# Eigenvectors of a normalised Laplacian inside a two-layer graph network: one twisted factorisation instead of two, three refinements instead of two, a shorter last QR sweep

## Chip, cores and metric

The kernel runs on 1 core of a Trainium2 chip. The metric is the device time of an execution in microseconds (us); lower is better.

## The reference, cut to what matters

Input are x (128 batches of 128 nodes by 128 features, f32) and one 128x128 adjacency matrix. The first layer needs the eigenvectors of its normalised Laplacian, with the signs that the library's routine gives them, the second is a graph convolution followed by LSTM cells over windows of 1 to 4 nodes:

```python
deg = jnp.sum(A, axis=0) + jnp.sum(A, axis=1) - jnp.diagonal(A)
d_inv_sqrt = jnp.where(deg > 0, jax.lax.rsqrt(deg), 0.0)
L_norm = d_inv_sqrt[:, None] * (jnp.diag(deg) - A) * d_inv_sqrt[None, :]
_, U = jnp.linalg.eigh(L_norm)
out = relu(jnp.einsum('mn,bnd->bmd', U.T, relu(layernorm(x))) @ W1 + b1) @ W2 + b2
x = x + jnp.einsum('nm,bmd->bnd', U, out)
# then layer norm, two mixing layers with adj, LSTM cells for p = 1..4, and a second residual sum
```

## The kernel before, in words

The program for each engine is written out by hand with semaphores; no planner sets the order. It has two halves. The second half, the batch part, runs over 128 batches in 8 rounds of 4 streams of 4 batches; its first matmul is L735, which waits for `eig_done`, and the diff does not touch it. The first half computes the eigenvectors U (and UT) for all batches at once:

- **Tridiagonal form.** 127 Householder steps (`householder(k, before)` on DVE, lines 910 to 972). A step is a chain over three engines: DVE makes the new row x (L963), PE spreads it over the partitions (L618, L620), ACT takes the square root of the sum of squares (L442) and half the absolute pivot (L443), DVE forms u (L926), PE multiplies it with A (L623, L625), and DVE computes the next row and updates A (L952 to L972). L930 copies the sum of squares, plus a tiny number, out of PSUM; `prepare_sign` (L979, L980) and `prepare_row` (L986) prepare the next step's sign vector. L986 stands behind the last update of A, L972. ACT fills its spare time with the layer norm's statistics.
- **The leaf's sign.** After 16 steps DVE hands the leading 16x16 block to POOL (`leaf_ready`). POOL runs 16 sweeps of a QR iteration on it, in a loop of 88 instructions (lines 335 to 416); each sweep looks for the active block (L347 to L364), computes a shift (L365 to L375), forms the pivots d - shift (L377), and multiplies the parity `PAR` by the sign of the first (L379, L383). A recurrence of 15 pairs L386, L388 follows, then products over 16 elements (L390 to L415), with one long `pow` at L403. At each turn the loop clears its semaphore. Only `PAR` is used afterwards: L417 passes it to DVE with `leaf_sign`.
- **Eigenvalues and vectors.** DVE, beside POOL, runs two Sturm counts (L1120 to L1151) and then `twisted` twice: a factorisation from both ends for 4 levels of splitting at once, 127 steps of small instructions (L1203, L1209), and then wide instructions over 4 levels of 128 elements (L1212 to L1255). The first call corrects the eigenvalues by a Rayleigh quotient (L1245, L1259 to L1262), the second gives the vectors V4.
- **Refinement.** The vectors are turned back by PE (L608 to L709) and refined twice against the Laplacian (L1291 to L1340), PE and DVE in turn. The signs follow from V4 and from POOL's parity: in the last refinement DVE waits for `leaf_sign` before L1360, forms the row of signs in M[9] (L1363), applies the last step (L1366) and the signs (L1369 to L1385). L1382 and L1385 release the batch part.
- **PE and ACT in between** build the product of reflectors, turn the LSTM weights, and normalise and multiply x by W1 in place; they end before DVE's vectors. ACT's L517 waits for DVE's L1266.

Semaphore waits of one engine are in order: what stands behind a waiting instruction waits with it.

Of the kernel before, what the change touches and what calls it, by code (L numbers as in the profile page):

```python
# [19 lines left out]
TINY = 1e-30  # L20
QR_PER = 88
RAYLEIGH_CLIP = 4e-5
REGULAR = 1e-12
REFINES = 2

# [34 lines left out]
def build(nc, t_in, out):  # L60
    with ExitStack() as ctx:
# [117 lines left out]
        rs_out = sem("rs_out")  # L179
        st1, st2, tw1, tw2 = sem("st1"), sem("st2"), sem("tw1"), sem("tw2")  # L180
        pool_s = sem("pool_s")
# [19 lines left out]
        def half_x(k):  # L201
            return sc[:, 28 + k % 2:29 + k % 2]
# [98 lines left out]
        def _(pool):  # L301
# [33 lines left out]
            TS = nc.gpsimd.tensor_scalar  # L335
            with nc.gpsimd.Fori(0, QR_SWEEPS) as k:
                pool.sem_clear(pool_q)
                q = Tally(pool_q)

                def op(ins):  # L340
                    q.did(ins)
                    q.last(pool)

                def go(ins):
                    return q.did(ins)

                go(TT(y16[:, 0:15], d16[:, 0:15], d16[:, 1:16], ALU.mult))  # L347
# [27 lines left out]
                op(TT(SIG, SIG, S(OG), ALU.subtract))  # L375

                op(TS(am, d16, SIG, 1e-15, ALU.subtract, ALU.add))  # L377

                go(TS(T0, am[:, 0:1], 0.0, -2.0, ALU.is_ge, ALU.mult))  # L379
                n_par = q.n  # L380
                n_rho = go(TT(rho[:, 0:1], am[:, 0:1], neg16[:, 0:1], ALU.pow))
# [33 lines left out]
                op(TT(d16[:, LEAF - 1:LEAF], SIG, gam[:, LEAF - 1:LEAF], ALU.add))  # L415
                assert q.n == QR_PER, q.n
            nc.gpsimd.tensor_copy(S(PAR), S(PAR)).then_inc(leaf_sign, 1)  # L417
            pool.wait_ge(ln_var, 3)
# [4 lines left out]
        def _(act):  # L423
# [15 lines left out]
            for k in range(STEPS):  # L439
                t = k + 1  # L440
                act.wait_ge(s_ready, k + 1)
                nc.scalar.activation(two_sigma(k), banks[7][:, 1:2], ACT.Sqrt, scale=4.0).then_inc(sigma_ready, 1)  # L442
                nc.scalar.activation(half_x(k), banks[7][:, 0:1], ACT.Abs, scale=0.5).then_inc(sigma_ready, 1)  # L443
                act.wait_ge(a_ready, k + 1)
                nc.scalar.activation(S_(ACOL), A[:, t:t + 1], ACT.Copy, scale=below[:, t:t + 1]).then_inc(acol_ready, 1)
                if t + 1 < N:
                    act.wait_ge(xb_ready, k + 1)
                    nc.scalar.activation(uB[:, k % 2, t + 1:N], banks[0][:, t + 1:N], ACT.Copy).then_inc(row_ready, 1)
                act.wait_ge(sg_ready, k + 1)
                act.wait_ge(sigma_ready, 2 * k + 1)  # L450
# [149 lines left out]
        def _(pe):  # L600
# [116 lines left out]
            for r in range(REFINES):  # L717
                mms((B[3], Lap[:], U[:]))
                also((B[5], U[:], U[:]))
                mms((B[6], ones[:], V4[:, 1, :]))  # L720
                mms((B[4], U[:], M[0]))
                mms((B[1], ones[:], M[2]))
                if r == REFINES - 1:
                    mms((banks[0][:, 0:2 * N], ones[:], diag2))
                mms((B[3], UT[:], M[5]))
                also((B[2], M[5], UT[:]))
# [118 lines left out]
        def _(dve):  # L845
# [66 lines left out]
            def householder(k, before):  # L912
# [8 lines left out]
                sigma2, sg = two_sigma(k), sign(k)  # L921
                x_t, s = banks[7][:, 0:1], banks[7][:, 1:2]

                dve.wait_ge(sigma_ready, 2 * k + 1)
                dve.wait_ge(hv, before)
                V.scalar_tensor_tensor(out=u_c, in0=S(SGE), scalar=sigma2, in1=x_c,  # L926
                                       op0=ALU.mult, op1=ALU.add).then_inc(u_ready, 1)

                dve.wait_ge(sigma_ready, 2 * k + 2)
                n_st = step(V.tensor_scalar(S(ST), s, TINY, None, ALU.add))  # L930
                V.tensor_scalar(sg, x_t, 0.0, 0.5, ALU.is_ge, ALU.subtract).then_inc(sg_ready, 1)
                dve.wait_ge(hv, n_st)
                n_den = step(V.scalar_tensor_tensor(out=S(DEN), in0=half_x(k), scalar=sigma2, in1=S(ST),
# [12 lines left out]
                if t + 1 < N:  # L946
# [22 lines left out]
                                                   in1=banks[1][:, live(k)], op0=ALU.mult, op1=ALU.subtract))  # L969
                n_sge1 = prepare_sign(k + 1) if k + 1 < STEPS else None  # L970
                dve.wait_ge(hv, max(n_a, n_wb))
                V.scalar_tensor_tensor(out=A[:, live(k)], in0=wB[:, live(k)], scalar=S(HU), in1=A[:, live(k)],  # L972
                                       op0=ALU.mult, op1=ALU.add).then_inc(a_ready, 1)
                return prepare_row(k + 1, n_sge1) if k + 1 < STEPS else None

            def prepare_sign(k):

                dve.wait_ge(x_ready, k + 1)
                n_sge1 = step(V.tensor_scalar(S(SGE1), ident[:, N:N + 1], 0.0, 0.5, ALU.is_ge, ALU.subtract))  # L979
                step(V.tensor_tensor(UC[:, k, 1:2], ident[:, N:N + 1], below[:, k + 1:k + 2], ALU.mult))  # L980
                return n_sge1

            def prepare_row(k, n_sge1):
# [4 lines left out]
            before = prepare_row(0, prepare_sign(0))  # L988
            for k in range(LEAF):
# [195 lines left out]
            TWO = [slice(0, 2), slice(2, 4)]  # L1185
            LEAST, GSUM, NORM, INV, RQ = 56, 60, 20, 24, 36


            def twisted(sem, vectors):
                for l in range(LEVELS):  # L1190
# [47 lines left out]
                for l in range(LEVELS):  # L1238
# [3 lines left out]
                                                      ALU.mult, ALU.add))  # L1242
                for l in range(LEVELS):
                    if not vectors:
                        go(V.tensor_tensor_reduce(out=GAM[:, l, :], in0=GAM[:, l, :], in1=ONE[:, l, :], scale=1.0,  # L1245
                                                  scalar=0.0, op0=ALU.mult, op1=ALU.add, accum_out=S(GSUM + l)))
                for h in TWO:
# [9 lines left out]
                t.last(dve)  # L1257
                if not vectors:
                    op(V.reciprocal(S(RQ, LEVELS), S(NORM, LEVELS)))  # L1259
                    op(V.tensor_tensor(S(RQ, LEVELS), S(RQ, LEVELS), S(GSUM, LEVELS), ALU.mult))  # L1260
                    op(V.tensor_scalar(S(RQ, LEVELS), S(RQ, LEVELS), RAYLEIGH_CLIP, -RAYLEIGH_CLIP, ALU.min, ALU.max))
                    op(V.tensor_tensor(lam4[:], lam4[:], S(RQ, LEVELS), ALU.add))  # L1262

            twisted(tw1, False)
            twisted(tw2, True)
            V.tensor_copy(S(41), S(NORM)).then_inc(rs_in, 1)  # L1266
            n_31 = go(V.scalar_tensor_tensor(out=S(31), in0=ident[:, 64:65], scalar=wrow[:, 0, 64:65], in1=ident[:, 63:64],
                                             op0=ALU.mult, op1=ALU.add))
            largest = tell(V.tensor_tensor(S(30), lam4[:, 0:1], ident[:, N - 1:N], ALU.mult))  # L1269
            CC, ZZ, LF, SIGN, LFA, LFB = 44, 47, 50, 54, 55, 40  # L1270
            for l in range(LEVELS - 1):
# [19 lines left out]
            for r in range(REFINES):  # L1291
# [50 lines left out]
                if r == 0:  # L1342

                    op(V.tensor_tensor(S(ZZ, 3), S(ZZ, 3), S(INV + 1, 3), ALU.mult))
                    go(V.tensor_scalar(S(ZZ, 3), S(ZZ, 3), S(43), None, ALU.is_le))
                    go(V.tensor_scalar(S(CC, 3), S(CC, 3), 0.0, None, ALU.is_lt))
                    go(V.tensor_scalar(S(LF), V4[:, 0, 0:1], 0.0, None, ALU.is_gt))
                    op(V.tensor_scalar(S(LF + 1), V4[:, 0, 0:1], 0.0, None, ALU.is_lt))
                    for l in (2, 1, 0):
# [176 lines left out]
```

## Time and profile before

| | before |
|---|---|
| median of 3 runs | 1515.49 us (1513.96 to 1518.14) |
| the profiled execution | 1516.81 us, span 1515.1 us |
| busy share PE / DVE / ACT / POOL | 79% / 73% / 62% / 34% |
| granted TensorE clock, mean | 0.939 |
| span until the batch part's first matmul | 660.71 us |

The span runs from the first to the last instruction; the execution's own time includes what lies around it. Shares are averages over two halves that are bound by different engines: in the first PE is seldom busy, in the second almost always. An instruction's row gives its start, its duration and, in brackets, how long its engine had been idle and who released it.

### The profile page before, as it was taken

The page shows a single profiled execution, that of the slowest core. Times are in us where ns is not written, and L with a number is a line of the kernel's source. Part 1 is how long each engine was busy: PE and PEld are TensorE (multiplying, and loading weights), DVE is VectorE, ACT ScalarE, POOL GpSimd, SP SyncE. Part 2 cuts the span into 40 slices and gives each one's busy share as a digit, 9 for nine tenths or more (in the row PEclk, how much of TensorE's full clock was granted, in tenths as well). Part 3 has the DMA queues.
Part 4 walks back from the last instruction along what each step waited for, and adds up shares of the span by engine and source line. Part 5 has one row for each costly group of instructions (what it writes and reads, how often), then busy time and mean ns, then how long its engine had stood idle before and what let it go on. Part 6 is the DMA issues. An engine that isn't in the chain of part 4 may idle for free.

```text
span 1515.1 us, 26850 instructions
## 1 busy us (share of the span) xinstructions
PE 1196.2 (79%) x7121; PEld 1069.9 (71%) x7121; DVE 1107.1 (73%) x5944; ACT 943.2 (62%) x3339; POOL 508.6 (34%) x1426
## 2 busy tenths in 40 slices
PE   5777777777536400179999999999999999999998
PEld 4566666666435300168789899898998989989897
DVE  8999999999999999958747656455564554645545
ACT  4666666666349600012478687786877868778676
POOL 0288888888888888830000200000000000000000
PEclk9999999999869855579999999999999999999999
DMA  9300000000000000003100000000000000000001
GB/s 269 79 1 1 1 1 1 1 1 1 1 1 1 1 0 0 1 28 105 36 1 2 28 0 28 0 0 28 0 28 0 0 28 0 26 2 0 28 1 29
DMA packets 43630, 28.80 MB, mean 19 GB/s; under 512 B 1520, under 2 KB 39440, under 8 KB 43536
## 3 DMA queue, kind: packets, MB, share of 16 engines
q1 hardware_dynamic: 43536, 27.81, 6.7%
q14 instruction: 67, 0.55, 0.1%
q8 instruction: 27, 0.44, 0.1%
HBM read 19.42 MB, written 8.39 MB: 18 GB/s over the span
## 4 chain that ended last, share of the span: by engine, by line
PE 52%; POOL 33%; issue 7%; DVE 6%; ACT 2%; POOLq 0%; ACTq 0%; DVEq 0%
PE bank L815 13%; PE bank L805 10%; POOL leaf L388 9%; PE bank L810 8%; PE bank L818 7%; POOL leaf L386 6%; POOL leaf L403 3%; PE bank L735 2%; PE bank L787 2%; PE bank L779 2%; PE bank L743 2%; PE bank L773 2%; PE bank L750 2%; PE bank L758 2%; ACT BIG L552 1%
## 5 line engine op out<-in xcount | busy, mean ns | idle before, releaser
L815 PE MATMUL bank<-spare,wT 128*128 128x256 f32 (+2 forms) x1408 | 311.3, 321 | 0.0
L552 ACT ACTIVATE PV<-bank,bias 128x256 f32<-128x256 f32 (+2 forms) x704 | 304.0, 435 | 0.0
L552 ACT ACTIVATE BIG<-bank,bias 128x128 f32<-128x128 f32 (+2 forms) x544 | 227.6, 418 | 121.0 <-PE bank L818 101.9
L815 PEld LDWEIGHTS bank<-spare,wT 128*128 128x128 f32 x1408 | 234.8, 191 | 13.2
L805 PE MATMUL bank<-spare,wT 128*128 128x128 f32 (+2 forms) x1088 | 228.1, 320 | 4.1 <-DVE spare L1446 2.7
L1432 DVE TENSOR_TENSOR BIG<-BIG,PV 128x128 f32<-128x128 f32 (+2 forms) x192 | 63.0, 328 | 205.9 <-ACT BIG L552 205.9
L805 PEld LDWEIGHTS bank<-spare,wT 128*128 128x128 f32 x1088 | 168.7, 190 | 22.5 <-DVE spare L1446 9.1
L818 PE MATMUL bank<-spare,wT 128*128 128x128 f32 (+2 forms) x768 | 169.7, 303 | 0.0
L810 PE MATMUL bank<-spare,wT 128*128 128x128 f32 (+2 forms) x768 | 141.6, 307 | 3.8 <-DVE spare L1444 1.4
L618 PE MATMUL bank<-ident 128*128 128x2 f32 x254 | 74.3, 362 | 88.6 <-DVE ident L963 87.5
L388 POOL TENSOR_TENSOR leaf<-leaf 128x1 f32<-128x1 f32 x240 | 136.7, 570 | 20.0
L560 ACT ACTIVATE spare<-spare 128x256 f32<-128x256 f32 (+2 forms) x352 | 134.4, 382 | 6.9 <-DVE spare L1435 6.9
L618 PEld LDWEIGHTS bank<-ident 128*128 128x128 f32 x254 | 63.6, 311 | 99.6 <-DVE ident L963 98.2
L1429 DVE TENSOR_TENSOR spare<-BIG,PV 128x256 f32<-128x256 f32 (+2 forms) x160 | 60.8, 380 | 95.7 <-ACT PV L552 95.6
L818 PEld LDWEIGHTS bank<-spare,wT 128*128 128x128 f32 x768 | 125.2, 191 | 3.3
L810 PEld LDWEIGHTS bank<-spare,wT 128*128 128x128 f32 x768 | 113.8, 191 | 14.2 <-DVE spare L1444 10.9
L386 POOL TENSOR_SCALAR leaf<-leaf 128x1 f32<-128x1 f32 x240 | 93.3, 389 | 23.4
L610 PE MATMUL bank<-ones,sc 128*128 128x1 f32 x2 | 0.6, 348 | 120.5 <-DVE sc L1269 120.5
L442 ACT ACTIVATE sc<-bank 128x1 f32<-128x1 f32 x127 | 21.7, 171 | 116.1 <-PE bank L618 116.0
L623 PE MATMUL bank<-A,UC 128*128 128x127 f32 (+63 forms) x254 | 87.5, 442 | 7.3 <-DVE UC L926 0.8
L1209 DVE SCALAR_TENSOR_TENSOR PV<-RC,m,PV 128x4 f32<-128x4 f32 x508 | 90.6, 220 | 0.0
L610 PEld LDWEIGHTS bank<-ones,sc 128*128 128x128 f32 x2 | 0.5, 313 | 120.6 <-issue 120.6
(405 smaller groups left out, 3000.8 us busy)
## 6 DMA issues: line engine op xcount, KB each, us to landing
spare<-in_x SPq DMA_DIRECT2D x32, 256.0 KB, 3.8
out<-X SPq DMA_DIRECT2D x32, 256.0 KB, 2.4
spare<-in_L_gnn_Wih SPq DMA_DIRECT2D x4, 256.0 KB, 5.2
spare<-in_L_gnn_Whh SPq DMA_DIRECT2D x4, 256.0 KB, 4.6
W<-in_L_gnn_W SPq DMA_DIRECT2D x2, 64.0 KB, 2.7
Wg<-in_L_gnn_Wg SPq DMA_DIRECT2D x2, 64.0 KB, 2.4
adj<-in_adj SPq DMA_DIRECT2D x1, 64.0 KB, 2.0
X<-in_x SPq DMA_DIRECT2D x4, 0.5 KB, 17.0
```

Of the source, the lines that this page charges most:

```text
L386: op(TS(am[:, i + 1:i + 2], rho[:, i:i + 1], ne16[:, i:i + 1], am[:, i + 1:i + 2], ALU.mult, ALU.add))
L388: op(TT(rho[:, i + 1:i + 2], am[:, i + 1:i + 2], neg16[:, 0:1], ALU.pow))
L552: last = nc.scalar.activation(gate_out[q][i][:, 0:T], gate(i, q, T), ACT.Tanh if q == GATE_G else ACT.Sigmoid, bias=bias[:, at:at + 1])
L560: nc.scalar.activation(tS[i][:, 0:T], cS[i][:, 0:T], ACT.Tanh).then_inc(tanh_ready[i], 1)
L618: nc.tensor.matmul(banks[7][:, 0:2], x_wide, ident[:, t:N + 1:N - t], start=True, stop=True).then_inc(s_ready, 1)
L623: nc.tensor.matmul(banks[1][:, live(k)], u_c.to_broadcast([N, N]), A[:, live(k)], start=True, stop=True).then_inc(pb_ready, 1)
L805: last = nc.tensor.matmul(gate(i, q, T), wT[:, 0, p - 1, q * D:(q + 1) * D], xt, start=True, stop=(j == 0))
L810: last = nc.tensor.matmul(gate(i, q, T), wT[:, 1, p - 1, q * D:(q + 1) * D], hS[i][:, 0:T], start=False, stop=True)
L815: last = nc.tensor.matmul(gate(i, q, T), wT[:, 0, p - 1, q * D:(q + 1) * D], xt, start=True, stop=(j == 0))
L818: last = nc.tensor.matmul(gate(i, q, T), wT[:, 1, p - 1, q * D:(q + 1) * D], hS[i][:, 0:T], start=False, stop=True)
L1209: s.did(V.scalar_tensor_tensor(out=nx, in0=RC[:, last + lane:last + lane + live], scalar=M[2][:, row:row + 1], in1=nx, op0=ALU.mult, op1=A ...
L1432: V.tensor_tensor(gI[i][:, 0:T], gI[i][:, 0:T], gG[i][:, 0:T], ALU.mult).then_inc(cell_part[i], 1)
```

## The change

- POOL's 16 sweeps are written out instead of looped, and the last ends after its shift: it computes the first pivot alone and its sign, and the final product of `PAR` signals `leaf_sign`.
- In a Householder step ACT makes the copy of the sum of squares (`S(ST)`) as its third instruction, L930 on DVE goes, and DVE waits for all three ACT results before L931. The sign vector for the next step (L986) is formed before the last update of A, not behind it.
- `twisted` runs once, without the Rayleigh correction, and there are three refinements. A new scalar `LINKED` (whether the first split is coupled) masks the last test of the signs, through a third block in the diagonal matrix that PE spreads, and the test's threshold is 0 instead of 1e-4.

```diff
-REFINES = 2
+REFINES = 3
...
-            with nc.gpsimd.Fori(0, QR_SWEEPS) as k:
-                pool.sem_clear(pool_q)
-                q = Tally(pool_q)
...
+            for k in range(QR_SWEEPS):
                 go(TT(y16[:, 0:15], d16[:, 0:15], d16[:, 1:16], ALU.mult))
...
+                if k == QR_SWEEPS - 1:
+                    op(TS(am[:, 0:1], d16[:, 0:1], SIG, 1e-15, ALU.subtract, ALU.add))
+                    op(TS(T0, am[:, 0:1], 0.0, -2.0, ALU.is_ge, ALU.mult))
+                    break
                 op(TS(am, d16, SIG, 1e-15, ALU.subtract, ALU.add))
...
-            nc.gpsimd.tensor_copy(S(PAR), S(PAR)).then_inc(leaf_sign, 1)
+            TS(S(PAR), T0, 1.0, S(PAR), ALU.add, ALU.mult).then_inc(leaf_sign, 1)
...
                 nc.scalar.activation(half_x(k), banks[7][:, 0:1], ACT.Abs, scale=0.5).then_inc(sigma_ready, 1)
+                nc.scalar.activation(S_(ST), banks[7][:, 1:2], ACT.Copy, bias=TINY).then_inc(sigma_ready, 1)
...
-                act.wait_ge(sigma_ready, 2 * k + 1)
+                act.wait_ge(sigma_ready, 3 * k + 1)
...
                 if r == REFINES - 1:
-                    mms((banks[0][:, 0:2 * N], ones[:], diag2))
+                    mms((banks[0][:, 0:3 * N], ones[:], diag3))
...
-                dve.wait_ge(sigma_ready, 2 * k + 2)
-                n_st = step(V.tensor_scalar(S(ST), s, TINY, None, ALU.add))
+                dve.wait_ge(sigma_ready, 3 * k + 3)
                 V.tensor_scalar(sg, x_t, 0.0, 0.5, ALU.is_ge, ALU.subtract).then_inc(sg_ready, 1)
-                dve.wait_ge(hv, n_st)
...
-                n_sge1 = prepare_sign(k + 1) if k + 1 < STEPS else None
+                following = prepare(k + 1) if k + 1 < STEPS else None
                 dve.wait_ge(hv, max(n_a, n_wb))
                 V.scalar_tensor_tensor(out=A[:, live(k)], in0=wB[:, live(k)], scalar=S(HU), in1=A[:, live(k)],
                                        op0=ALU.mult, op1=ALU.add).then_inc(a_ready, 1)
-                return prepare_row(k + 1, n_sge1) if k + 1 < STEPS else None
-
-            def prepare_sign(k):
+                return following
+
+            def prepare(k):
...
-            twisted(tw1, False)
-            twisted(tw2, True)
+
+            twisted(tw)
...
                 if final:
-                    go(V.tensor_scalar(diag2[:, 0:N], I, S(LFA), None, ALU.mult))
-                    signs = tell(V.tensor_scalar(diag2[:, N:2 * N], I, S(LFB), None, ALU.mult))
+                    go(V.tensor_scalar(diag3[:, 2 * N:3 * N], I, S(LINKED), None, ALU.mult))
+                    go(V.tensor_scalar(diag3[:, 0:N], I, S(LFA), None, ALU.mult))
+                    signs = tell(V.tensor_scalar(diag3[:, N:2 * N], I, S(LFB), None, ALU.mult))
...
                     op(V.tensor_tensor(S(ZZ, 3), S(ZZ, 3), S(INV + 1, 3), ALU.mult))
+                    op(V.tensor_scalar(S(LINKED), S(ZZ), S(43), None, ALU.is_gt))
...
-                else:
+                elif final:
                     hear(signs)
...
+                    go(V.tensor_tensor(S(TEST), S(SIGN), S(LINKED), ALU.mult))
+                    op(V.tensor_tensor(M[8], banks[0][:, 2 * N:3 * N], M[9], ALU.mult))
...
-            n_r = go(V.tensor_tensor(M[2], B[6], M[9], ALU.mult))
+            n_r = go(V.tensor_tensor(M[2], B[6], M[8], ALU.mult))
...
-            n_c = go(V.tensor_tensor(S(53), banks[5][:, 0:1], S(SIGN), ALU.mult))
+            n_c = go(V.tensor_tensor(S(53), banks[5][:, 0:1], S(TEST), ALU.mult))
```

## Rows read from the trace of the kernel before

**Rows 1.** The page, part 4: the chain that ended last, shares of the span by engine.
```profile
PE 52%; POOL 33%; issue 7%; DVE 6%; ACT 2%; POOLq 0%; ACTq 0%; DVEq 0%
```

**Rows 2.** List of waits to 661 us: engine, line, waited for: total, times, longest.
```profile
ACT sc L517 <- DVE sc L1266: 119.5, 1, 119.5
DVE sc L1360 <- POOL leaf L417: 3.4, 1, 3.4
```

**Rows 3.** Timeline, POOL: start us, us, engine, line, operation, xcount [idle before].
```profile
64.31 0.21 POOL L347 TENSOR_TENSOR leaf<-leaf 128x15 f32<-128x15 f32 x1 [0.25 <-POOL leaf L333]
...
580.02 0.21 POOL L347 TENSOR_TENSOR leaf<-leaf 128x15 f32<-128x15 f32 x1 [0.46 <-POOL leaf L415]
...
625.22 1.31 POOL L377 TENSOR_SCALAR leaf<-leaf 128x16 f32<-128x16 f32 x1
...
657.87 0.18 POOL L417 COPY leaf<-leaf 128x1 f32<-128x1 f32 x1 [0.23 <-POOL leaf L415]
```

**Rows 4.** The chain in order of time: start us, us, what; POOL's L403, one a sweep.
```profile
95.58 2.78 POOL leaf L403
...
575.30 2.79 POOL leaf L403
610.98 2.79 POOL leaf L403
...
653.37 2.79 POOL leaf L403
```

**Rows 5.** Groups of POOL: count, busy us, mean ns of one, idle us before.
```profile
L379 POOL TENSOR_SCALAR leaf<-leaf 128x1 f32<-128x1 f32 x16 | 4.3, 270 | 1.4
```

**Rows 6.** Timeline of one early Householder step, DVE and, last, PE.
```profile
18.35 0.34 DVE L972 SCALAR_TENSOR_TENSOR A<-wB,sc,A 128x126 f32<-128x126 f32 x1
18.61 0.15 DVE L986 TENSOR_TENSOR sc<-sc,ident 128x1 f32<-128x1 f32 x1
18.87 0.22 DVE L926 SCALAR_TENSOR_TENSOR UC<-sc,ident 128x1 f32<-128x1 f32 x1
19.00 0.15 DVE L930 TENSOR_SCALAR sc<-bank 128x1 f32<-128x1 f32 x1
19.19 0.22 DVE L933 SCALAR_TENSOR_TENSOR sc<-sc 128x1 f32<-128x1 f32 x1
19.97 0.22 DVE L952 SCALAR_TENSOR_TENSOR sc<-bank,sc 128x1 f32<-128x1 f32 x1
...
19.14 0.79 PE L623 MATMUL bank<-A,UC 128*128 128x125 f32 x2
```

**Rows 7.** Timeline, DVE: second factorisation's first, L1266 after its last, last refinement's first and last.
```profile
560.28 0.34 DVE L1191 TENSOR_SCALAR PV<-D,lam 128x128 f32<-128x128 f32 x1
...
635.70 0.15 DVE L1266 COPY sc<-sc 128x1 f32<-128x1 f32 x1
...
648.13 0.29 DVE L1297 TENSOR_TENSOR U<-U,bank 128x128 f32<-128x128 f32 x1
...
654.44 0.28 DVE L1358 COPY m<-bank 128x128 f32<-128x128 f32 x1
```

**Rows 8.** Timeline, POOL: L386 beside factorisation's start, in the quiet stage, beside refinements.
```profile
560.58 1.46 POOL L386 TENSOR_SCALAR leaf<-leaf 128x1 f32<-128x1 f32 x1
...
590.76 0.33 POOL L386 TENSOR_SCALAR leaf<-leaf 128x1 f32<-128x1 f32 x1
...
596.27 0.34 POOL L386 TENSOR_SCALAR leaf<-leaf 128x1 f32<-128x1 f32 x1
...
636.24 0.56 POOL L386 TENSOR_SCALAR leaf<-leaf 128x1 f32<-128x1 f32 x1
...
648.28 0.34 POOL L386 TENSOR_SCALAR leaf<-leaf 128x1 f32<-128x1 f32 x1
```

**Rows 9.** Timeline, DVE: the first instruction behind L1363.
```profile
658.60 0.29 DVE L1366 TENSOR_TENSOR U<-U,bank 128x128 f32<-128x128 f32 x1
```

**Rows 10.** Windows, 660 to 665 us: busy of each engine, PEclk, DMA share, GB/s.
```profile
660.00:665.00 5.00, 4.29 (x20) 4.29 (x21) 1.01 (x7) 1.16 (x2) 0.00 (x0) 0.50 0.00 0
```

More of the change, by code:

```diff
@@ L20 @@
 TINY = 1e-30
-QR_PER = 88
-RAYLEIGH_CLIP = 4e-5
 REGULAR = 1e-12
-REFINES = 2
+REFINES = 3
 BATCH, D = 128, 128
@@ L179, in build @@
         rs_out = sem("rs_out")
-        st1, st2, tw1, tw2 = sem("st1"), sem("st2"), sem("tw1"), sem("tw2")
+        st1, st2, tw = sem("st1"), sem("st2"), sem("tw")
         pool_s = sem("pool_s")
@@ L237, in build @@
         DOUBLINGS = 6
-        diag2 = BIG[:, 5 * GW:5 * GW + 2 * N]
+        diag3 = BIG[:, 5 * GW:5 * GW + 3 * N]
         def squares_done(e):
@@ L335, in _, with go @@
             TS = nc.gpsimd.tensor_scalar
-            with nc.gpsimd.Fori(0, QR_SWEEPS) as k:
-                pool.sem_clear(pool_q)
-                q = Tally(pool_q)
[L340 to L345, printed above, removed]
+            def go(ins):
+                return q.did(ins)
+            for k in range(QR_SWEEPS):
                 go(TT(y16[:, 0:15], d16[:, 0:15], d16[:, 1:16], ALU.mult))
@@ L375, in _ @@
                 op(TT(SIG, SIG, S(OG), ALU.subtract))
+                if k == QR_SWEEPS - 1:
+                    op(TS(am[:, 0:1], d16[:, 0:1], SIG, 1e-15, ALU.subtract, ALU.add))
+                    op(TS(T0, am[:, 0:1], 0.0, -2.0, ALU.is_ge, ALU.mult))
+                    break
                 op(TS(am, d16, SIG, 1e-15, ALU.subtract, ALU.add))
-                go(TS(T0, am[:, 0:1], 0.0, -2.0, ALU.is_ge, ALU.mult))
-                n_par = q.n
+                n_par = go(TS(T0, am[:, 0:1], 0.0, -2.0, ALU.is_ge, ALU.mult))
                 n_rho = go(TT(rho[:, 0:1], am[:, 0:1], neg16[:, 0:1], ALU.pow))
@@ L415, in _ @@
                 op(TT(d16[:, LEAF - 1:LEAF], SIG, gam[:, LEAF - 1:LEAF], ALU.add))
-                assert q.n == QR_PER, q.n
-            nc.gpsimd.tensor_copy(S(PAR), S(PAR)).then_inc(leaf_sign, 1)
+            TS(S(PAR), T0, 1.0, S(PAR), ALU.add, ALU.mult).then_inc(leaf_sign, 1)
             pool.wait_ge(ln_var, 3)
@@ L921, in householder @@
                 sigma2, sg = two_sigma(k), sign(k)
-                x_t, s = banks[7][:, 0:1], banks[7][:, 1:2]
-                dve.wait_ge(sigma_ready, 2 * k + 1)
+                x_t = banks[7][:, 0:1]
+                dve.wait_ge(sigma_ready, 3 * k + 1)
                 dve.wait_ge(hv, before)
@@ L980, in prepare_sign @@
                 step(V.tensor_tensor(UC[:, k, 1:2], ident[:, N:N + 1], below[:, k + 1:k + 2], ALU.mult))
-                return n_sge1
-            def prepare_row(k, n_sge1):
                 dve.wait_ge(hv, n_sge1)
                 return step(V.tensor_tensor(S(SGE), S(SGE1), ident[:, k + 1:k + 2], ALU.mult))
-            before = prepare_row(0, prepare_sign(0))
+            before = prepare(0)
             for k in range(LEAF):
@@ L1185, in _, with twisted @@
             TWO = [slice(0, 2), slice(2, 4)]
-            LEAST, GSUM, NORM, INV, RQ = 56, 60, 20, 24, 36
-            def twisted(sem, vectors):
+            LEAST, NORM, INV = 56, 20, 24
+            def twisted(sem):
                 for l in range(LEVELS):
@@ L1242, in twisted @@
                                                       ALU.mult, ALU.add))
[L1243 to L1246, printed above, removed]
                 for h in TWO:
@@ L1257, in twisted @@
                 t.last(dve)
[L1258 to L1262, printed above, removed]
-            twisted(tw1, False)
-            twisted(tw2, True)
+            twisted(tw)
             V.tensor_copy(S(41), S(NORM)).then_inc(rs_in, 1)
@@ L1269, in _ @@
             largest = tell(V.tensor_tensor(S(30), lam4[:, 0:1], ident[:, N - 1:N], ALU.mult))
-            CC, ZZ, LF, SIGN, LFA, LFB = 44, 47, 50, 54, 55, 40
+            CC, ZZ, LINKED, LF, SIGN, LFA, LFB, TEST = 44, 47, 37, 50, 54, 55, 40, 38
             for l in range(LEVELS - 1):
@@ L1373, in _ @@
             hear(by_row)
-            n_r = go(V.tensor_tensor(M[2], B[6], M[9], ALU.mult))
+            n_r = go(V.tensor_tensor(M[2], B[6], M[8], ALU.mult))
             hear(by_col)
-            n_c = go(V.tensor_tensor(S(53), banks[5][:, 0:1], S(SIGN), ALU.mult))
+            n_c = go(V.tensor_tensor(S(53), banks[5][:, 0:1], S(TEST), ALU.mult))
             dve.wait_ge(v_, n_r)
-            n_r = go(V.tensor_scalar(M[2], M[2], 1e-4, -2.0, ALU.is_gt, ALU.mult))
+            n_r = go(V.tensor_scalar(M[2], M[2], 0.0, -2.0, ALU.is_gt, ALU.mult))
             dve.wait_ge(v_, n_c)
-            n_c = go(V.tensor_scalar(S(53), S(53), 1e-4, -2.0, ALU.is_gt, ALU.mult))
+            n_c = go(V.tensor_scalar(S(53), S(53), 0.0, -2.0, ALU.is_gt, ALU.mult))
             dve.wait_ge(v_, n_r)
```

## The prediction, made before the changed kernel was run

> **What bounds the kernel now.** I read the chain of waits first: PE holds 52% of it and POOL 33% [rows 1]. In the part before 661 us (the eigenvectors) the reader is to see that POOL, not DVE, is last. DVE is busy almost without a break there, but the list of waits shows that it stood 3.4 us before L1360 until POOL's L417 gave it the leaf's sign [rows 2]. So the two engines run side by side and POOL ends 3.4 us later: taking work from DVE alone gains nothing. ACT waited 119.5 us for DVE's L1266, so it has slack. After L1382 everything is the batch part, bound by PE; the diff does not touch it, so it moves as one block with the moment at which U is ready.
>
> POOL's timeline gives its chain: it starts with DVE's leaf values, the first sweep's L347 is at 64.31, the last sweep passes L377 at 625.22, and L417 ends at 658.05 (657.87 + 0.18) [rows 3]. That is one serial chain of 16 sweeps.
>
> **The change, part by part.**
>
> 1. **Last sweep only to its pivot.** What ran from L377's start to L417's end, 658.05 - 625.22 = 32.8 us, goes [rows 3]. In its place come three instructions on one element, each waiting for the one before: 3 x 270 ns, the mean of L379, plus two gaps of 0.09 us (1.4 us of idle time over 16) [rows 5], 1.0 us. **-31.8 us**, all on the path.
>
> 2. **Sweeps written out.** At each turn of the loop POOL stands 0.46 us before L347 [rows 3], where a dependent instruction stands 0.09 [rows 5]. 15 x 0.37 = **-5.6 us**. Ends: 0, if the 0.46 is not the branch and the semaphore clear; +4.6 if fresh code costs something. For the latter the trace has one hint: the loop's first pass, whose code has never run, took 31.27 us from L347 to L403 (64.31 to 95.58), a later quiet one 30.96 (580.02 to 610.98) [rows 3, 4]; 0.31 x 15 = 4.6. I take the full gain, since the first pass also ran beside Householder steps. The Trainium skill (Runtime: NRT & Kernel Launch, Instruction fetch mechanics) says that instructions stream in blocks of 16 KiB whose crossing is mostly hidden, and that a taken branch is what disturbs this; by it the full gain stands too, and its "mostly" is what the slow rival below would need.
>
> 3. **Householder steps.** POOL starts after 16 of them; the other 111 run on DVE beside POOL and are worth nothing at the end. In an early step [rows 6] L986 starts 0.26 after L972 and L926 0.26 after that. With L986 put ahead of L972, it costs its short issue slot (some 0.1) and L926 follows L972 at 0.26: about 0.14 earlier. With L930 on ACT, DVE's L933 no longer waits for it: it can start 0.07 behind L931 rather than 0.19 behind L930, 0.12 sooner. But PE's L623 ends at 19.93 and L952 starts at 19.97: PE moves with L926 only, so 0.14 is kept. ACT's new copy issues behind L442 and L443 and ends about when L931 could start. I take 0.13 a step, 16 x 0.13 = **-2.1 us**. Ends: -4.2 (0.26 a step, both gains), and +1.0 if DVE now waits 0.06 a step for ACT's third result.
>
> 4. **One twisted factorisation less, one refinement more.** On DVE the removed one is 635.70 - 560.28 = 75.4 us, about as the second; a refinement is 654.44 - 648.13 = 6.3 us and 0.9 for PE's product [rows 7], which the next one has nothing to cover with. DVE would then be ready for the sign at 654.7 - 75.4 + 7.2 = 586, and at some 570 with all 127 steps shorter. POOL's new end is 620, so DVE now waits 35 to 50 us at L1360: this part is worth **0 by itself**, hidden by POOL. ACT's work before L517 keeps at least 119.5 - 75.4 - 16 = 28 us of slack.
>
> 5. **What DVE's wide instructions do to POOL.** In a quiet stage (DVE on 4-element instructions) a pair L386, L388 takes (596.27 - 590.76) / 5 = 1.10 us; beside the refinement (648.28 - 636.24) / 10 = 1.20 [rows 8]. The sweep that met the second factorisation's wide end and the refinements took 653.37 - 610.98 = 42.4 us against 35.7 before it [rows 4]: 6.7 lost, 1.0 of it beside refinements, so 5.7 to the factorisation's end. In the sum so far, all that was lost after 625 went with term 1. Now the surviving sweeps meet the one factorisation end as before, not the second one's set-up (L386 took 1.46 instead of 0.34 at 560.58, -1.1 [rows 8]), and all of the preparation and three refinements, 27 us x 0.09 = +2.4. **+1.3 us.** Ends: -1, and +11 (27 us at the end-stage's rate, 5.7 in 12). I take the rate of the refinement itself, since it is the same work. The Trainium skill (SBUF — State Buffer, Who interferes with whom) has a rule against this change: a DVE instruction with two SBUF inputs and a GpSimd instruction that reads SBUF exclude each other for a whole instruction. By that rule alone the added refinement would cost POOL up to several us; the rows above show 1.2 us lost for 12 us of refining.
>
> 6. **Tail after the sign.** L1363 is followed by a product with the new PSUM columns (0.29, as L1366 [rows 9], with a gap and the TEST product in front), all on the path: **+0.4 us**. LINKED and the third diagonal lie in DVE's slack.
>
> 7. **PE's clock.** From 660 to 665 the granted clock was 0.50 with PE busy 4.3 of 5 us [rows 10], that is 1.2 GHz at the start of the batch part. PE will now have stood longer before it, but it is already at the low level: 0. Ends: -1 and +2, by when the clock rises.
>
> Sum: -31.8 - 5.6 - 2.1 + 1.3 + 0.4 = **-37.8 us**. The profiled execution took 1516.81 us for a span of 1515.1; it gives 1479.0. The median of the runs, 1515.49, is 1.3 lower: **1477.7 us**.
>
> **Rivals.**
> - *Denser DVE work stalls POOL*: the sweeps beside the refinements lose at the rate of the factorisation's end, +9.7 over term 5: 1487. For: single POOL instructions reach 1.46 [rows 8]; against: the 1.20 a pair.
> - *The change does less than it says*: turn gap and Householder order give nothing: -31.8 + 1.3 + 0.4 = -30.1: 1485. For: the 0.46 is only attributed to the turn, and PE, ACT and DVE are nearly tied in a step [rows 6].
> - *DVE becomes last*: it would need 35 us more on DVE, and the floor of its own path is 658.1 - 586 = 72 us below today's: 1443. Only if POOL's written-out sweeps were much quicker.
> - *Slower than before, by POOL's written-out code*: POOL is the bound, and a sweep has 74 waits, 15 x 74 + 25 = 1135 in all. If fresh code stretched each gap of 0.09 by half, that is +51 us: 1529. It decides from 38 / 1135 = 0.033 us a wait. For: POOL has never run written-out code of this length here. Against: the loop's first pass, 0.31 us slower for 74 waits, and DVE's own written-out stream.
>
> **How the numbers follow.** A measurement of this kernel can tell about 0.3%, 4.5 us. The forecast case (POOL's chain, terms near those taken, 1472 to 1483) gets 0.69; denser stalls 0.13; less than it says 0.12; DVE last 0.01; an outcome below 1472 with POOL still last 0.02; slower 0.03. The range 1470 to 1488 leaves out the two far rivals and part of the stalls. The likeliest case gives 1477.7. Faster 0.96, same 0.01 (1511 to 1520, stalls of 2.5 us a sweep), slower 0.03.
>
> **What would show it.** In the profile after: L1360 waits for POOL 35 to 50 us (not 3.4); PE, ACT and DVE idle there together; POOL's turn gap 0.1 instead of 0.46; 15 long instructions like L403, not 16; POOL's first sweep at about 62; pairs at 1.2 us beside the refinements; the sign about 38 us earlier, with U used 0.4 later behind it. I am wrong if DVE does not wait for POOL there, if POOL's quiet sweep is not near 35.2 us, or if the batch part changes its length by more than 2 us.

## The result and the profile after

The changed kernel takes 1475.43 us (median of 4 runs, 1474.63 to 1475.85), the kernel before 1516.34 (4 runs, 1513.96 to 1518.14): ratio 0.9732, 95% interval 0.9720 to 0.9744, 40.9 us less. Forecast were 1477.7 us and a range of 1470 to 1488.

| | before | after |
|---|---|---|
| profiled execution, span | 1516.81, 1515.1 us | 1475.44, 1473.7 us |
| busy share PE / DVE / ACT / POOL | 79 / 73 / 62 / 34% | 81 / 70 / 64 / 33% |
| granted TensorE clock, mean | 0.939 | 0.949 |
| batch part's first matmul | 660.71 us | 620.29 us |
| from there to the end | 854.4 us | 853.4 us |

Part 4 of the page after, the chain that ended last, answers to [rows 1]:

```profile
PE 52%; POOL 32%; issue 6%; DVE 3%; ACT 2%; ACTq 0%; DVEq 0%; POOLq 0%
```

Shares hardly move, although the span lost 41 us: POOL still sets the end of the first half. The list of waits says it more sharply (engine, line, waited for: total, times, longest), and answers to [rows 2]:

```profile
POOL leaf L328 <- DVE leaf L989: 59.2, 1, 59.2
ACT sc L511 <- DVE sc L1244: 42.1, 1, 42.1
DVE sc L1340 <- POOL leaf L410: 41.6, 1, 41.6
```

L1340 is the old L1360: DVE waits 41.6 us for the sign where it waited 3.4. The removed factorisation and the shorter steps have become idle time on DVE. The windows show that stretch, with columns PE, PEld, DVE, ACT, POOL busy, PEclk, DMA share, GB/s; the second line is the start of the batch part, which answers to [rows 10]:

```profile
576.00:617.00 41.00, 0.72 (x4) 0.42 (x2) 0.00 (x0) 0.00 (x0) 33.83 (x107) 0.50 0.00 0
620.00:625.00 5.00, 4.71 (x29) 4.71 (x30) 0.58 (x3) 1.63 (x3) 0.00 (x0) 0.66 0.00 0
```

For 41 us next to nothing but POOL works. Its timeline after (start, duration, ...), to be laid beside [rows 3, 4]:

```profile
62.21 0.21 POOL L338 TENSOR_TENSOR leaf<-leaf 128x15 f32<-128x15 f32 x1
...
602.85 2.77 POOL L397 TENSOR_TENSOR leaf<-leaf 128x15 f32<-128x15 f32 x1
...
606.93 0.19 POOL L409 TENSOR_TENSOR leaf<-leaf 128x1 f32<-128x1 f32 x1
607.20 0.21 POOL L338 TENSOR_TENSOR leaf<-leaf 128x15 f32<-128x15 f32 x1
...
616.24 0.30 POOL L369 TENSOR_SCALAR leaf<-leaf 128x1 f32<-128x1 f32 x1
616.63 0.23 POOL L370 TENSOR_SCALAR leaf<-leaf 128x1 f32<-128x1 f32 x1
616.97 0.27 POOL L410 TENSOR_SCALAR leaf<-leaf 128x1 f32<-128x1 f32 x1
```

L397 is the old L403, and there are 15 of it. The gap at the turn is 607.20 - 607.12 = 0.08 us where it was 0.46. Behind the last turn only the shift and three one-element instructions are left. On DVE the sign is followed by the tail:

```profile
617.27 0.22 DVE L1340 SCALAR_TENSOR_TENSOR sc<-sc,leaf 128x1 f32<-128x1 f32 x1 [41.63 <-POOL leaf L410]
617.41 0.34 DVE L1343 SCALAR_TENSOR_TENSOR m<-bank,leaf,m 128x128 f32<-128x128 f32 x1
617.79 0.16 DVE L1345 TENSOR_TENSOR sc<-sc 128x1 f32<-128x1 f32 x1
617.87 0.28 DVE L1346 TENSOR_TENSOR m<-bank,m 128x128 f32<-128x128 f32 x1
618.18 0.29 DVE L1348 TENSOR_TENSOR U<-U,bank 128x128 f32<-128x128 f32 x1
```

Laid end to end, the two traces close the account. The time at which POOL starts its first sweep's L347/L338: 64.31 to 62.21, **-2.1**. The first sweep up to its long `pow`: 31.27 to 31.75, **+0.5**. From the first `pow` to the fifteenth: 515.40 to 508.89, **-6.5**. From the fifteenth to the end of the sign (L417 before, L410 after): 47.07 to 14.39 (602.85 to 617.24), **-32.7**. From the sign to the first batch matmul: 2.66 to 3.05, **+0.4**. Batch part: **-1.0**. Together -41.4, and the spans differ by 41.4.

### The profile page after: what moved, and what is told of

It reads as the page before. It is cut to its first block, busy times and chain, and to the rows that moved or that the text cites. A ratio compares the mean times of both kernels' runs of the same rounds, so it can differ in the third digit from the quotient of the medians.

```text
span 1473.7 us, 26229 instructions
## 1 busy us (share of the span) xinstructions
PE 1197.3 (81%) x7135; PEld 1072.9 (73%) x7135; DVE 1029.8 (70%) x5271; ACT 948.9 (64%) x3466; POOL 479.5 (33%) x1370
## 4 chain that ended last, share of the span: by engine, by line
PE 52%; POOL 32%; issue 6%; DVE 3%; ACT 2%; ACTq 0%; DVEq 0%; POOLq 0%
PE bank L809 13%; PE bank L799 10%; POOL leaf L382 9%; PE bank L804 8%; PE bank L812 7%; POOL leaf L380 6%; POOL leaf L397 3%; PE bank L729 2%; PE bank L781 2%; PE bank L773 2%; PE bank L737 2%; PE bank L767 2%; PE bank L744 2%; PE bank L752 2%; ACT BIG L546 1%
## 5 line engine op out<-in xcount | busy, mean ns | idle before, releaser
L382 POOL TENSOR_TENSOR leaf<-leaf 128x1 f32<-128x1 f32 x225 | 125.9, 560 | 18.8
L527 ACT ACTIVATE PV<-bank,b 128x512 f32<-128x512 f32 x32 | 22.0, 687 | 129.0 <-PE bank L729 129.0
L380 POOL TENSOR_SCALAR leaf<-leaf 128x1 f32<-128x1 f32 x225 | 84.6, 376 | 21.9
L614 PE MATMUL bank<-ident 128*128 128x126 f32 (+62 forms) x252 | 84.1, 431 | 0.0
L617 PEld LDWEIGHTS bank<-A,UC 128*128 128x128 f32 x254 | 63.5, 310 | 24.9 <-DVE UC L920 24.9
```

The source lines that it names most:

```text
L380: op(TS(am[:, i + 1:i + 2], rho[:, i:i + 1], ne16[:, i:i + 1], am[:, i + 1:i + 2], ALU.mult, ALU.add))
L382: op(TT(rho[:, i + 1:i + 2], am[:, i + 1:i + 2], neg16[:, 0:1], ALU.pow))
L614: nc.tensor.matmul(banks[0][:, t + 1:N], x_wide, ident[:, t + 1:N], start=True, stop=True).then_inc(xb_ready, 1)
L617: nc.tensor.matmul(banks[1][:, live(k)], u_c.to_broadcast([N, N]), A[:, live(k)], start=True, stop=True).then_inc(pb_ready, 1)
```

## The experiments

Every kernel was timed in turn with the kernel before, each in several rounds; ratios are against that. Differences between two variants are differences of such ratios, times about 1518 us.

**1. All but the twisted factorisation's part (e_not4).** POOL's code and the Householder steps as after, but two factorisations and two refinements:

```diff
 REFINES = 2
-            twisted(tw)
+            twisted(tw1, False)
+            twisted(tw2, True)
```

> The change without its part 4: two factorisations and two refinements as before, POOL's sweeps and the Householder steps as after. My theory (two chains side by side, the later one sets the end): DVE would be ready for the sign at 575.6 + 75.4 - 7.2 = 644 us, behind POOL's 617, so DVE is last and the time is 1475.4 + 26.6 - 0.4 = 1501.6 us; DVE's wait for POOL at the sign is gone. Rival (part 4 is worth nothing in this change, as it is hidden by POOL): 1475 us, with DVE waiting.

Measured: 1504.40 us, ratio 0.9912 [0.9895, 0.9928]. Against 1517.45 us before on the same chip that is 13 us won, and 27 less than the full change wins (0.9912 - 0.9732, times 1518). The page's chain and DVE's timeline:

```profile
PE 59%; DVE 31%; ACT 3%; issue 2%; ACTq 0%; DVEq 0%
```

```profile
645.13 0.28 DVE L1348 COPY m<-bank 128x128 f32<-128x128 f32 x1
645.33 0.21 DVE L1350 SCALAR_TENSOR_TENSOR sc<-sc,leaf 128x1 f32<-128x1 f32 x1
645.46 0.34 DVE L1353 SCALAR_TENSOR_TENSOR m<-bank,leaf,m 128x128 f32<-128x128 f32 x1
```

POOL is gone from the chain, and L1350 (the old L1360) has no waiting time in front: DVE is last. The 13 us are the 3.4 it used to wait [rows 2], and about 10 us of shorter Householder steps: the instruction behind the last one starts at 370.5 in this trace and at 380.1 before.

**2. Only that part (e_only4).** The kernel before with `twisted` once, three refinements and the signs' new form.

```diff
-            twisted(tw1, False)
-            twisted(tw2, True)
+            twisted(tw)
-REFINES = 2
+REFINES = 3
```

> The kernel before with part 4 alone: one factorisation, three refinements; looped full sweeps and Householder steps as before. My theory: POOL stays last and only what DVE's wide instructions do to it changes: the second factorisation's end no longer meets the last sweep (-6.7), its set-up goes (-1.1), the refinements move ahead (+2.4), the tail grows (+0.4): -5.0, some 1511 us, DVE waiting about 65 us. Rival (DVE's work does not slow POOL, part 4 fully hidden): 1516.7. Rival (DVE's chain is what counts): 1447.

Measured: 1512.20 us, ratio 0.9963 [0.9949, 0.9977], 5 us won. Waits, and the last steps of POOL's chain:

```profile
DVE sc L1351 <- POOL leaf L416: 68.4, 1, 68.4
POOL leaf L346 <- POOL leaf L414: 6.9, 15, 0.5
```

```profile
577.79 2.79 POOL leaf L402
613.24 2.78 POOL leaf L402
648.42 2.79 POOL leaf L402
```

The last sweep takes 648.42 - 613.24 = 35.2 us; in the kernel before it took 42.4, beside the second factorisation's end and the refinements [rows 4]. So DVE's removed work gave 65 us of idle time on DVE and a quiet last sweep on POOL. **The two halves of the change win 13 and 5 us alone and 41 together**: each engine's cut only pays when the other is cut too.

**3. The whole last sweep (e_full).**

```diff
-                if k == QR_SWEEPS - 1:
-                    op(TS(am[:, 0:1], d16[:, 0:1], SIG, 1e-15, ALU.subtract, ALU.add))
-                    op(TS(T0, am[:, 0:1], 0.0, -2.0, ALU.is_ge, ALU.mult))
-                    break
...
-            TS(S(PAR), T0, 1.0, S(PAR), ALU.add, ALU.mult).then_inc(leaf_sign, 1)
+            nc.gpsimd.tensor_copy(S(PAR), S(PAR)).then_inc(leaf_sign, 1)
```

> After with a whole last sweep, written out. My theory: all of it lies on POOL's chain beside an idle DVE, so a quiet sweep's remainder: 35.3 - 9.0 + the final copy - the three short ones = +25.5 us, 1501 us. Before's trace had 32.8 us there, since it met DVE's wide instructions. Rival (the last sweep is hidden in part by DVE or by the start of the batch part): less than +15.

Measured: 1500.98 us, ratio 0.9892 [0.9875, 0.9908]. DVE's wait grows by the same amount:

```profile
DVE sc L1336 <- POOL leaf L406: 66.5, 1, 66.5
```

66.5 - 41.6 = 24.9 us. In the changed kernel the cut is worth 24 to 25 us (24 by the ratios), not the 32 of term 1: the other 6 to 7 us are the slow end of the old last sweep, which the missing factorisation alone removes, as the second experiment shows.

**4. The sweeps looped again (e_loop).** Fifteen whole sweeps in a loop, the short last one written out behind it.

```diff
-            for k in range(QR_SWEEPS):
+            with nc.gpsimd.Fori(0, QR_SWEEPS - 1) as k:
+                pool.sem_clear(pool_q)
+                q = Tally(pool_q)
```

> After with 15 sweeps looped again, the last shortened sweep written out behind the loop. My theory: each turn costs 0.38 us more again and the start 0.2: +5.8 us, 1481.2 us. Rival (written-out code wins nothing, or loses what fresh code costs): 1475 or below.

Measured: 1482.09 us, ratio 0.9768 [0.9751, 0.9784], about 5 us over the changed kernel's 0.9732 to 0.9736. The waits of the turn:

```profile
POOL leaf L345 <- POOL leaf L412: 6.4, 14, 0.5
```

14 turns at 0.46 us against 0.08 are 5.3 us. This shows that the gap was the turn of the loop (its branch and the semaphore clear together, which no run parts), and that the written-out code costs nothing that takes the gain away.

**5. Both Householder edits undone (e_house), and the copy alone (e_st).** In e_house `prepare_sign` and `prepare_row` stand where they were and DVE makes the copy; in e_st only the copy goes back:

```diff
-                nc.scalar.activation(S_(ST), banks[7][:, 1:2], ACT.Copy, bias=TINY).then_inc(sigma_ready, 1)
...
-                dve.wait_ge(sigma_ready, 3 * k + 3)
+                dve.wait_ge(sigma_ready, 2 * k + 2)
+                n_st = step(V.tensor_scalar(S(ST), s, TINY, None, ALU.add))
                 V.tensor_scalar(sg, x_t, 0.0, 0.5, ALU.is_ge, ALU.subtract).then_inc(sg_ready, 1)
+                dve.wait_ge(hv, n_st)
```

> After with both Householder edits undone (L930's copy back on DVE, L986 behind the update of A). Only 16 of the 127 steps lie on POOL's chain. My theory: 16 x 0.13 = +2.1 us, 1477.5, POOL's first instruction at 63.35 instead of 61.41 and all 127 steps 16 us longer on DVE's side, hidden. Rival (the ACT copy or the order costs elsewhere, or all steps count): 1475 or 1491.

> After with only the copy of the sum of squares back on DVE; L986 stays ahead of the update of A. My theory: PE's L623 and DVE's row of small instructions nearly tie in the early steps, so the copy alone gives under half: POOL starts 0 to 1 us later than in after, 1475.4 to 1476.4. Rival (the copy is the part that pays, 0.12 a step): +1.9, 1477.3.

The changed kernel was run once more as a control (c_after):

> The changed kernel itself once more, as the control beside the next two on one chip, and to see how far POOL's chain repeats. My theory: ratio to before 0.973 as before, POOL's sweeps beside the same code within 1 to 4 us in total, since which of its instructions meets a wide one of DVE is a matter of chance.

It gave 1479.39 us (1474.64 to 1479.71), ratio 0.9736 [0.9722, 0.9749]: one and the same kernel differs by 5 us between its executions. Measured: e_house 1484.61 us, 0.9771 [0.9757, 0.9784]; e_st 1479.13 us, 0.9736 [0.9723, 0.9749]. So the two edits are worth 0.0035, 5 us with an uncertainty of some 3, and the copy alone nothing that can be told. e_house and e_st ran on one chip and lie 5.5 us apart, with the order of L986 as the only edit between them. The start moves as term 3 said. The waits of e_house and of e_st before POOL's first instruction:

```profile
POOL leaf L328 <- DVE leaf L994: 61.1, 1, 61.1
```

```profile
POOL leaf L328 <- DVE leaf L990: 59.3, 1, 59.3
```

61.1 against 59.2 after is 1.9 us for 16 steps, and e_st has 1.8 of them: it is the order of L986 that moves the start, not ACT's copy. The rest of the 5 us lies in POOL's sweeps: from the first long `pow` to the fifteenth e_house took 515.66 us and e_st 511.57. Five kernels with both edits and the same work beside POOL (after, c_after, e_full, e_warm, e_warm6) took 508.3 to 513.3 us, so this stretch scatters by 5 us for no edit at all. e_house lies 2.3 us above all of them; whether the order of L986 slows POOL's sweeps is not settled. On DVE's side the two edits are worth less than expected: DVE's last instruction before its wait for the sign, the copy out of PSUM, starts at 584.55 instead of 575.36, 9 us later and not 16.

**6. Three more refinements (e_ref6).**

```diff
-REFINES = 3
+REFINES = 6
```

> After with six refinements instead of three (the output is the same to rounding). DVE gets 3 x 7.2 = 21.6 us more, half of its 41.6 us of waiting; what can change the time is only the slowing of POOL. My theory: 1.19 us a pair beside refinements against 1.08 to 1.10, 9 to 10%, so 21.6 x 0.09 = +2.0 us, 1477.4. Rival (wide instructions stall POOL as at the factorisation's end, 5.7 in 12 us): +10, 1485. Rival (no effect): 1475.4.

Measured: 1480.48 us, ratio 0.9747 [0.9732, 0.9761]; the difference of 0.0011 (1.7 us) to the control is inside the intervals. The trace shows both halves of it (waits; then the chain):

```profile
DVE sc L1340 <- POOL leaf L410: 21.6, 1, 21.6
```

```profile
567.50 2.79 POOL leaf L397
604.22 2.79 POOL leaf L397
```

Three refinements take 41.6 - 21.6 = 20.0 us of DVE's idle time, 6.7 each, and that sweep lasts 36.72 us instead of 35.29: 1.4 us for 20 us of refining, 7%. By the trace a refinement is as good as free here.

**7. PE kept awake (e_warm, e_warm6).** Some idle matmuls of 512 columns, whose product nothing reads, run before the sign; they add work, they leave none out. e_warm has ten, e_warm6 six:

```diff
+            pe.wait_ge(pool_q, 4 + 88 * (QR_SWEEPS - 1) + 10)
+            for _ in range(WARM):
+                nc.tensor.matmul(banks[7][:], ones[:], X[:, 0:GB, :], start=True, stop=True)
             mms((B[6], sc[:, 32:33].to_broadcast([N, N]), U[:]))
```

> After with ten matmuls of 512 columns on PE, on numbers that nothing uses, released when POOL is in its last, shortened sweep; they change no output. Before the batch part the clock is at 0.50 and rises only 3.1 us after L729 has begun, so this stretch runs at half speed. My theory: with PE busy just before, the clock is at 1.0 when L729 begins: L729's group takes 3.6 us instead of 5.3, -1.7 us, and the final test's products are shorter by some 0.3: 1473.4. Rival (the extra matmuls end too late or the clock falls again in the pause before L729): 1475.4 or more.

> As e_warm, with six matmuls instead of ten on numbers that nothing uses. In e_warm they ran 10.3 us and PE was not free when the sign came. My theory: six run about 7 us and end before the sign; L729's group takes 3.8 us as in e_warm instead of 5.3: 1.5 us less than the control, with DVE's wait for the sign unchanged. Rival (the clock falls again in the 2 to 4 us before L729): equal to the control.

Measured: e_warm 1479.51 us, 0.9735 [0.9722, 0.9748], a miss; e_warm6 1477.15 us, 0.9725 [0.9712, 0.9739], 2.2 us under the control's median with overlapping intervals, so that the timing does not show the 1.5 us. PE in e_warm, then in e_warm6:

```profile
614.26 10.27 PE L724 MATMUL bank<-X,ones 128*128 128x512 f32 x20 [37.08 <-POOL leaf L347]
624.36 0.38 PE L605 MATMUL bank<-U,sc 128*128 128x128 f32 x2
```

```profile
610.09 8.46 PE L724 MATMUL bank<-X,ones 128*128 128x512 f32 x12 [33.12 <-POOL leaf L347]
618.63 0.49 PE L605 MATMUL bank<-U,sc 128*128 128x128 f32 x2
618.96 0.28 PE L704 MATMUL bank<-sc,U 128*128 128x1 f32 x2
620.27 3.84 PE L733 MATMUL bank<-U,X 128*128 128x128 f32 x32 [1.03 <-DVE U L1368]
```

The first batch group takes 3.84 us in both, against 5.32 after. Ten matmuls take 10.3 us and end so late that the sign's own product, L605, starts behind them: 2.8 us after POOL's last instruction (621.56) where it took 1.3 in e_warm6 (617.35). These 1.5 us take back what the first batch group gains. That e_warm's span is 5.7 us above e_warm6's has a second cause, which the ten matmuls can't have: POOL had its sign 4.2 us later, and it had lost these before PE's matmuls began, 2.3 between its first long `pow` and the eighth and 1.2 in the sweep that meets one long DVE instruction (see the last section).

**8. DVE takes over from POOL (e_hand, e_both).** POOL stops after 14 sweeps (`HAND`); DVE, idle by then, does the fifteenth and the short sixteenth with the same steps, its `reciprocal` in place of POOL's power of -1, and ACT takes the square root. e_both adds six idle matmuls, released from inside DVE's sweep.

```diff
-            for k in range(QR_SWEEPS):
+            for k in range(HAND):
...
                     dve.wait_ge(leaf_sign, 1)
+                    for k in range(HAND, QR_SWEEPS):
+                        go(V.tensor_tensor(y16[:, 0:15], d16[:, 0:15], d16[:, 1:16], ALU.mult))
...
+                            op(V.reciprocal(rho[:, i + 1:i + 2], am[:, i + 1:i + 2]))
```

> After with POOL stopping after 14 sweeps and DVE, which stood idle for 41.6 us, doing the last whole sweep and the shortened one itself, with the same formulas (its own reciprocal for x^-1, ACT's square root). My theory: POOL's 14th sweep ends at 572, DVE is free at 575.6; a dependent small instruction of DVE takes 0.18 to 0.25 us in its rows, so a sweep takes some 16 us and the short one 6: sign at 598 instead of 617, 19 us less than the control, 1457. Rival (DVE's small dependent instructions on the leaf are no quicker than POOL's, or ACT's square root costs several us): within 5 us of the control.

> e_hand and e_warm6 together: DVE does the last two sweeps, and PE runs six matmuls on numbers that nothing uses, released 9 us before DVE has the sign. My theory: the two gains add, 5.6 us for the first batch group in e_hand becomes 3.8: -1.8 us, ratio to before 0.9583 against 0.9595 for e_hand. Rival (PE is late or cold again): 0.9595 or above.

Measured: e_hand 1457.36 us, ratio 0.9595 [0.9581, 0.9608]; e_both 1457.47 us, 0.9598 [0.9585, 0.9611]. **e_hand is the fastest kernel of this study**, 4.05% below the kernel before and 22 us below the control on its chip. The traces explain 18 of the 22: the end of the sign moves from 616.37 in the control to 598.73. The control's trace is of its fastest execution; POOL's scatter would account for the other 4, but no trace of a slower execution is there to show it. e_hand's own five runs, with DVE last, lie within 1.1 us, the control's within 5.1. Its timeline on DVE:

```profile
575.65 0.28 DVE L1338 COPY m<-bank 128x128 f32<-128x128 f32 x1
575.85 0.17 DVE L1343 TENSOR_TENSOR leaf<-leaf 128x15 f32<-128x15 f32 x1
...
592.91 0.17 DVE L1343 TENSOR_TENSOR leaf<-leaf 128x15 f32<-128x15 f32 x1
...
598.57 0.16 DVE L1415 SCALAR_TENSOR_TENSOR leaf<-leaf 128x1 f32<-128x1 f32 x1
```

DVE goes from L1338 to the sweep without a wait, and the sweep takes 592.91 - 575.85 = 17.1 us where POOL's quiet one takes 35.3. The engine that was idle is also the one that is twice as fast at this work. Part of that is the other operation: DVE's `reciprocal` takes 0.16 us where POOL's `pow` takes 0.55, 15 times in the recurrence, and 0.25 where the long one takes 2.77, together 8.4 of the 18.2 us. DVE is now last from end to end, though POOL's 14 sweeps end at 575.53, only 0.3 us before DVE needs them. e_both won nothing over it. PE there:

```profile
589.20 7.45 PE L724 MATMUL bank<-X,ones 128*128 128x512 f32 x12 [12.46 <-DVE leaf L1393]
599.75 0.49 PE L605 MATMUL bank<-U,sc 128*128 128x128 f32 x2 [3.10 <-DVE U L1429]
600.07 0.34 PE L704 MATMUL bank<-sc,U 128*128 128x1 f32 x2
601.38 6.49 PE L733 MATMUL bank<-U,X 128*128 128x128 f32 x32 [0.96 <-DVE U L1445]
```

The matmuls ended 3.1 us before L605, and the group took 6.49 us, longer than the 5.64 of e_hand: the clock had fallen back. In e_warm6 that pause was 0.1 us. The granted clock of e_both (last number but two), at the end of the matmuls, at L605 and at the group's start:

```profile
594.00:596.65 2.65, 2.65 (x7) 0.86 (x5) 2.24 (x16) 0.05 (x1) 0.00 (x0) 1.00 0.00 0
599.75:600.50 0.75, 0.67 (x4) 0.58 (x4) 0.71 (x4) 0.00 (x0) 0.00 (x0) 0.77 0.00 0
601.38:604.00 2.62, 2.62 (x12) 2.62 (x13) 0.30 (x2) 0.51 (x1) 0.00 (x0) 0.50 0.00 0
```

## Why the prediction was right, point by point

The forecast's case held: POOL stayed last, DVE waited 41.6 us (forecast 35 to 50), the turn gap went to 0.08 (0.1), fifteen long `pow` remained, the quiet sweep took 35.29 us (35.2), U came 0.4 us later behind the sign (0.4). The profiled execution lost 41.4 us where the sum said 37.8. The mechanism was right; that the sum came this close is in part luck, since single terms were off by 1 to 2 us, terms 1 and 4 shared their worth out wrongly, and the changed kernel itself spreads over 5 us. Term by term:

- **Term 1, the last sweep cut, -31.8.** Measured -32.7 between the fifteenth `pow` and the sign: -31.8 behind the shift, 0.4 for the last turn, and 0.5 that POOL lost before L377 in the kernel before. As a difference of the two traces it was right. As the worth of the edit it was not: e_full puts it at 24 to 25 us. The rest belongs to the factorisation that no longer slows POOL, which terms 4 and 5 did not credit; term 5 even said that it "went with term 1". The sum is the same, the attribution is not.
- **Term 2, written out, -5.6.** Right: 15 turns, 0.38 us each; undoing it costs 5 us. The end "+4.6 if fresh code costs something" fell: the first pass takes 31.75 us against 31.27 looped, but 31.65 in e_loop, which is looped too, and 31.40 in e_warm6, which is not. With it fell the slow rival, 1529 us. The Trainium skill (Runtime: NRT & Kernel Launch, Instruction fetch mechanics) calls the crossing of a block mostly hidden and names the taken branch as the thing to avoid; these runs agree, with 0.46 us at a turn, though that holds the semaphore clear as well.
- **Term 3, Householder steps, -2.1.** The start moved by 1.9 to 2.1 us, as said. ACT's copy gives 0.1 us of it: the order of L986 does the rest, and PE, ready at the same moment, lets no more through, as the step had it. But the timed worth of both edits is 5 us with some 3 of uncertainty; the 3 us over lie in POOL's sweeps and are not explained.
- **Term 4, "worth 0 by itself".** This step of the reasoning was the weak one, though the sum is right. The term is hidden by POOL only in the order in which I took the terms: the cuts on POOL reach the end only because it makes room for them on DVE. Removed from the full change it costs 27 us, added alone it gives 5. The term should have said: a floor. DVE's own path without it ends at 645, so no cut on POOL can win more than the 3.4 us of [rows 2] and what the Householder steps save on DVE, 13 us in all. The 111 steps that "are worth nothing at the end" are worth 7.7 us in that kernel (9.6 for all 127, 1.9 for the first 16). On DVE all 127 steps gave under 10 us where the term had 16, which is why DVE was ready at 575.6 and not at 570; the wait for the sign, 41.6 us, still lay inside 35 to 50.
- **Term 5, DVE on POOL, +1.3.** The rate was right: 1.19 us a pair beside the refinements (eleven pairs from 549.44 to 562.50 in the trace after), as forecast, and 7% in e_ref6. The term came out at -0.7 all the same (+0.5 in the first sweep, -1.2 in the other fourteen), because the chain met one long DVE instruction well rather than badly (below): the sweep that holds it took 35.46 us against 37.81, 2.0 of it beyond the turn. That was luck. The 2 us are within the 5 us by which POOL's chain scatters between kernels with the same code there, so they show nothing.
- **Term 6, +0.4.** Measured +0.39.
- **Term 7, the clock, 0.** Measured -1.0: the first batch group took 5.32 us instead of 6.26, with a granted clock of 0.66 in its first 5 us where [rows 10] have 0.50. It is inside the ends given. Since the same group took 5.5 to 6.4 us in c_after and e_st behind the same idle stretch, these runs can't tell it from chance.

The rivals "denser DVE work stalls POOL" and "does less than it says" fell by the pair's 1.19 us and by e_loop. "DVE becomes last" did not happen here, but it is what e_not4 and e_hand are; its 1443 us took DVE ready at 586, where term 4 itself had 570.

## What to carry to other kernels

Where two engines run side by side and end within a few us of each other, price each cut together with the other engine's own end: here 13 and 5 us alone, 41 together. When a change turns a bound into a long wait of another engine, ask whether the waiting engine can do the rest of the work; here that gave another 18 us by the traces and 22 by the medians. Work hidden under such a wait can be added nearly for free (a refinement, 0.5 us by the trace of e_ref6).

## What the hardware did that I had not expected

- **DVE's long product held the POOL instruction that came behind it, but not one that had started.** The 128x2048 product on DVE takes 2.3 us and comes twice in each kernel. In the kernel before (POOL, then DVE):

```profile
388.86 3.05 POOL L355 TENSOR_TENSOR leaf<-leaf 128x16 f32<-128x16 f32 x4
```

```profile
388.94 2.30 DVE L1120 TENSOR_TENSOR PV<-dB,XG 128x2048 f32<-128x2048 f32 x1
```

  Four instructions that take 1.10 us in the first sweep after the change take 3.05. In e_st one starts 0.14 us behind DVE's product and ends 0.14 us behind its end; it takes 0.29 us elsewhere:

```profile
382.40 2.30 POOL L339 TENSOR_SCALAR leaf<-leaf 128x15 f32<-128x15 f32 x1
```

```profile
382.26 2.30 DVE L1109 TENSOR_TENSOR PV<-dB,XG 128x2048 f32<-128x2048 f32 x1
```

  A long one is held as well. In e_warm the `pow`, which takes 2.77 us elsewhere, starts 0.4 us behind the product:

```profile
379.95 4.58 POOL L398 TENSOR_TENSOR leaf<-leaf 128x15 f32<-128x15 f32 x1
```

```profile
379.58 2.32 DVE L1112 TENSOR_TENSOR PV<-dB,XG 128x2048 f32<-128x2048 f32 x1
```

  After the change the first product starts while POOL's `pow` is already running, and only the instruction behind the `pow` waits, for 0.2 us:

```profile
378.34 2.77 POOL L397 TENSOR_TENSOR leaf<-leaf 128x15 f32<-128x15 f32 x1
```

```profile
379.21 2.29 DVE L1108 TENSOR_TENSOR PV<-dB,XG 128x2048 f32<-128x2048 f32 x1
```

  So POOL's chain is 2 us longer or shorter by where in its sweep that one instruction falls. With the sweeps written out, the sweep that meets the first product took 35.5 to 37.3 us in the six kernels where the `pow` was running, and 38.1 to 38.5 in the other five. The Trainium skill (SBUF — State Buffer, Who interferes with whom) calls the pair of ports that the two engines share an exclusive lock. The held POOL instructions agree with it (in all 14 traces, at both products). The last pair does not: held for POOL's whole instruction, the lock would have kept DVE's product from ending before 381.11 + 2.3 us, and it ended at 381.50.
- **The clock's rise at the start of the batch part** varies by itself: the first group of 32 matmuls took 5.32 to 6.49 us in the eleven kernels without the extra matmuls, whether PE had stood 41.8 us before U's product (5.32, after) or 3.1 (6.26, before), and 3.84 in the two where PE was busy to within 0.1 us of the sign's product. In e_both, where it had stood 3.1 us behind 7.45 us of matmuls, the granted clock went from 1.00 to 0.50 again before the group began.
- **POOL against DVE on tiny dependent work:** POOL's `pow` on 15 elements takes 2.79 us and on one element 0.56; a sweep of 88 such steps takes 35.3 us on POOL and 17.1 on DVE, which has `reciprocal` (0.25 and 0.16 us) in the place of `pow`.
